# Decay steps on a ring of their own, with output, projections and taps placed among them

## Time and profile before

| | us |
|---|---|
| median of 3 runs | 1593.89 (1591.78 to 1598.0) |
| the profiled execution | 1599.31 |
| its span, first to last instruction | 1597.2 |
| TensorE busy | 1466.8 (92%) |
| VectorE busy | 1269.4 (79%) |
| ScalarE busy | 966.6 (61%) |
| GpSimd busy | 654.2 (41%) |

### The profile page before, as it was taken

How to read it: one execution, slowest core, us unless ns; L and a number is a source line. 1 busy time by engine, 2 the same in 40 slices (tenths; PEclk the granted TensorE clock), 3 DMA queues, 4 the chain that set the end, 5 groups by cost and what they waited for, 6 DMA issues and landing times.

```text
span 1597.2 us, 29712 instructions
## 1 busy us (share of the span) xinstructions
PE 1466.8 (92%) x9736; PEld 1143.2 (72%) x9736; DVE 1269.4 (79%) x2138; ACT 966.6 (61%) x1729; POOL 654.2 (41%) x554
## 2 busy tenths in 40 slices
PE   6799999799999789999879999877699999999979
PEld 5666666666766666666576676545598998998979
DVE  2788888698899788989779889943568988998954
ACT  3665666566566566656375656542267888887840
POOL 0134344133447524435814344834024544454530
PEclk7899999999999999999999999977769999999989
DMA  5376567466667755667847667713168989998858
GB/s 189 130 220 218 195 209 242 130 227 209 214 220 249 231 184 195 222 207 240 265 139 232 219 204 233 253 39 108 38 185 282 298 288 300 297 299 276 255 195 268
DMA packets 239686, 343.55 MB, mean 215 GB/s; under 512 B 20761, under 2 KB 191399, under 8 KB 238512
## 3 DMA queue, kind: packets, MB, share of 16 engines
q1 hardware_dynamic: 226096, 299.48, 59.4%
q0 software_dynamic: 13440, 42.19, 7.3%
HBM read 177.65 MB, written 172.30 MB: 219 GB/s over the span
## 4 chain that ended last, share of the span: by engine, by line
PE 64%; DVE 16%; issue 7%; ACT 5%; SPq 3%; DMA 2%; another core or an unknown queue 2%; POOL 1%; DVEq 0%; ACTq 0%; POOLq 0%
PE bank L451 12%; PE bank L618 11%; PE bank L453 10%; PE bank L452 10%; PE bank L629 6%; DVE e L1144 4%; PE bank L817 3%; PE bank L605 3%; DVE m L1185 2%; PE bank L793 2%; ACT e L880 2%; PE bank L763 2%; DVE e L1181 1%; DVE ew_lo L1077 1%
## 5 line engine op out<-in xcount | busy, mean ns | idle before, releaser
L1542 POOL TENSOR_TENSOR ssq<-ssq,ysq 128x512 f32<-128x512 f32 x128 | 167.8, 1311 | 428.7 <-ACT ysq L951 427.2
L1144 DVE SCALAR_TENSOR_TENSOR e<-bank,scal,e 128x511 f32<-128x511 f32 (+2 forms) x384 | 286.2, 745 | 35.2 <-ACT e L946 26.2
L1625 POOL DMA_INDIRECT outputs<-hsw,x_rows x160 | 181.6, 1135 | 238.0 <-DVE hsw L1488 185.7
L451 PE MATMUL bank<-h_hi,wi_hi 128*128 128x512 f32 x512 | 229.8, 449 | 33.2 <-issue 15.1
L618 PE MATMUL bank<-e,wn 128*128 128x512 f32 x512 | 247.6, 607 | 12.3 <-DVE e L1181 12.3
L1529 POOL TENSOR_TENSOR wi_lo<-wi,wi_hi 128x512 fp32r<-128x512 f32 x128 | 164.8, 1288 | 107.8 <-ACT wi_hi L828 107.8
L452 PE MATMUL bank<-h_lo,wi_hi 128*128 128x512 f32 x512 | 206.5, 403 | 0.0
L453 PE MATMUL bank<-h_hi,wi_lo 128*128 128x512 f32 x512 | 206.4, 403 | 0.0
L946 ACT ACTIVATE e<-bank,scal 128x512 f32<-128x512 f32 x128 | 99.4, 777 | 165.0 <-PE bank L453 163.4
L959 ACT ACTIVATE e<-e 128x512 f32<-128x512 f32 x128 | 80.7, 630 | 170.6 <-DVE e L1144 170.0
L1077 DVE TENSOR_TENSOR ew_lo<-ew,ew_hi 128x864 fp32r<-128x864 f32 x160 | 168.5, 1053 | 14.8 <-ACT ew_hi L828 8.1
(11 more groups left out here) (232 smaller groups left out, 3444.5 us busy)
## 6 DMA issues: line engine op xcount, KB each, us to landing
grouped<-zeros_out SPq DMA_DIRECT2D x256, 520.0 KB
ew<-expert_w SPq DMA_DIRECT2D x160, 432.0 KB
wi<-in_w SPq DMA_DIRECT2D x128, 256.0 KB
x_rows<-grouped SPq DMA_DIRECT2D x160, 130.0 KB
wo<-out_w SPq DMA_DIRECT2D x128, 128.0 KB
got<-outputs SPq DMA_DIRECT2D x16, 768.0 KB, 4.3
seg_wb<-seg_const POOLq DMA_DIRECT2D x4, 2048.0 KB, 8.3
seg_wa<-seg_const POOLq DMA_DIRECT2D x4, 2048.0 KB
```

Source lines behind the costliest of these rows:

```text
L451: mm(out, w_hi, x_hi, start=first, stop=False)
L1144: v.scalar_tensor_tensor(dst[:, d:], src[:, 0:SEQ - d], taps(TAPS - 1 - d), dst[:, d:], ALU.mult, ALU.add).then_inc(S[done], 1)
L1542: g_.tensor_tensor(ssq[:, :], ssq[:, :], ysq[:, :], ALU.add).then_inc(S["ssq_done"], 1)
L1625: g_.indirect_dma_start(outputs, bass.IndirectOffsetOnAxis(x_rows[:, i % XD, EMB:EMB + 1].bitcast(U32), 0), y_rows[:, i % YD, :], None, bo ...
```

## The change

- The decay steps get a ring of three: banks 6, 2 and 3, and for the exps the buffers `seg_e`, which are the two halves of `m` and `xt`. They no longer touch `ebuf`. Step 0 on ScalarE waits for the last head products of the batch before (`ssm`), steps 1 and 2 on TensorE for `xt_done` and `y_skip`.
- Slot 33 of a batch (last y: its square on ScalarE and the last output product on TensorE) moves into the next batch's steps, before step 3. Square sums stay before step 5, without the wait for VectorE's reading, which moves to before step 8. `gather_out` moves to before step 6.
- Pair 0's x projection runs before step 6 (TensorE), its first tap before step 8 (ScalarE), its three taps before step 10 (VectorE), its gate projection before step 10. In batches 1 to 3 the state products are before step 14 and the mask before step 18; in batch 0 both come after the steps.
- Pair 1 as well: cast of its weights before step 11, x projection before step 21, first tap before step 24, taps before step 27.
- The weights of the next batch's pairs 0 and 1 are loaded, and pair 0's cast and split, in the last slots of the batch before; in batch 0 pair 0's cast is before step 3.
- `seg_wb` is loaded in slot 31 and waits for three of the four send buffers.
- In batch 0 TensorE's steps wait for all six B/C taps.

The core of the diff:

```diff
-SEG_BANKS = (6, 0, 1, 2, 3, 7, 4, 5)
+SEG_RING, SEG_BANKS = 3, (6, 2, 3)
+SEG_OUT, SEG_SUMS, SEG_HID, SEG_GATHER, SEG_TAP0, SEG_SQUARE, SEG_TAPS, SEG_GATE = 3, 5, 6, 6, 8, 8, 10, 10
+SEG_NEXT_IN, SEG_G, SEG_MASK, SEG_NEXT_HID, SEG_NEXT_TAP0, SEG_NEXT_TAPS = 11, 14, 18, 21, 24, 27
-SEGMENTS_AT = 28
+SEGMENTS_AT, SECOND_SEGMENTS_AT = 28, 31
...
+            seg_e = (m[:, 0:2, :, :].rearrange("p t h l -> p (t h l)"), m[:, 2:4, :, :].rearrange("p t h l -> p (t h l)"),
+                     xt[:, :, :].rearrange("p t l -> p (t l)"))
...
             # SP
-                for par in range(2):
-                    load_in(b, par, par)
+                if b == 0:
+                    for par in range(2):
+                        load_in(b, par, par)
                 for j in range(PAIRS):
                     if j + 2 < PAIRS:
                         load_in(b, j + 2, j % 2)
+                    elif b + 1 < BATCH:
+                        load_in(b + 1, j + 2 - PAIRS, j % 2)
...
             # TensorE, segment
-                if u >= RING:
-                    pe.wait_ge(S["seg_exp"], n - RING + 1)
+                if u == 1:
+                    pe.wait_ge(S["xt_done"], START["xt_done"] + b * PAIRS)
+                if u == 2:
+                    pe.wait_ge(S["y_skip"], START["y_skip"] + b * PAIRS)
+                if u >= SEG_RING:
+                    pe.wait_ge(S["seg_exp"], n - SEG_RING + 1)
...
             # TensorE, a batch (hidden and gating are the two projections, cut out of slot)
+                pe.wait_ge(S["bc_taps"], 2 * (TAPS - 1) * (b + 1))
...
                 for u in range(CHUNK):
+                    if u == SEG_OUT and b:
+                        slot(b - 1, PAIRS + 1, 1, do_hid=False, do_in=False, do_mid=False, do_out="last")
+                        beside(b - 1, PAIRS + 1)
+                    if u == SEG_SUMS and b:
+                        pe.wait_ge(S["xhat"], (BATCH if b == 1 else BATCH + b - 1) * KE)
+                        square_sums(b - 1)
+                    if u == SEG_HID:
+                        hidden(b, 0, 0)
+                    if u == SEG_GATE:
+                        gating(b, 0, 0)
+                    if u == SEG_G and b:
+                        state_products(b)
+                    if u == SEG_NEXT_HID:
+                        hidden(b, 1, 1)
                     segment(b, u)
+                if b == 0:
+                    state_products(b)
                 beside(b, 0)
+                pe.wait_ge(S["seg_exp"], (b + 1) * CHUNK)
+                slot(b, 1, 1, do_hid=False, do_out="")
...
             # ScalarE
                 for u in range(CHUNK):
+                    if u == SEG_OUT:
+                        if b:
+                            slot(b - 1, PAIRS + 1, 1, do_tap=False, do_in=False, next_in=False, take_out=False)
+                            beside(b - 1, PAIRS + 1)
+                        else:
+                            take_in(b, 0, 0)
+                    if u == SEG_GATHER and b:
+                        gather_out(b - 1)
+                    if u == SEG_TAP0:
+                        first_tap(b, 0, 0)
+                    if u == SEG_NEXT_IN:
+                        take_in(b, 1, 1)
+                    if u == SEG_NEXT_TAP0:
+                        first_tap(b, 1, 1)
                     segment(b, u)
...
             # VectorE
+                    if u == SEG_SQUARE and b:
                         mean_square(b - 1)
+                    if u == SEG_TAPS:
+                        slot(b, 0, 0, do_mid=False, finish=False)
+                    if u == SEG_MASK and b:
+                        mask(b)
+                    if u == SEG_NEXT_TAPS:
+                        slot(b, 1, 1, do_mid=False, finish=False)
                     segment(b, u)
+                if b == 0:
+                    mask(b)
...
             # GpSimd
-                    for t in range(HD):
+                    for t in range(3):
                         pool.wait_ge(S[f"sent{t}"], 16 * TOP_K * max(0, b - 1))
...
-                    slot(b, j, j % 2, next_in=j < PAIRS - 1, finish=j > 1)
+                    slot(b, j, j % 2, next_in=j < PAIRS - 1 or j == PAIRS - 1 and b + 1 < BATCH, finish=j > 1)
```

More of the change, by code:

```diff
@@ L275, in seg_bank @@
         def seg_bank(u):
-            return bank[SEG_BANKS[u % RING]]
+            return bank[SEG_BANKS[u % SEG_RING]]
         def seg_step(b, u):
@@ L586, in beside, with hidden, gating, slot @@
                     i.then_inc(S["rank_mm"], 1)
-            def slot(b, j, par, do_in=True, do_mid=True, do_out="mid"):
+            def hidden(b, j, par):
                 g = b * PAIRS + j
                 x = tokens(b)
[L592 to L599, removed]
+                pe.wait_ge(S["wi_lo"], START["wi_lo"] + g + 1)
+                pe.wait_ge(S["taps"], START["taps"] + (TAPS - 1) * g)
+                for k in range(KE):
+                    w = slice((KE + k) * P, (KE + k + 1) * P)
+                    i = split_mm(p_hid[:, :], wi_hi[:, par, w], wi_lo[:, par, w], h_hi[:, k, x], h_lo[:, k, x],
+                                 k == 0, k == KE - 1)
+                i.then_inc(S["hid"], 1)
+            def gating(b, j, par):
+                g = b * PAIRS + j
+                x = tokens(b)
+                pe.wait_ge(S["silu_g"], START["silu_g"] + g)
+                for k in range(KE):
+                    w = slice(k * P, (k + 1) * P)
+                    i = split_mm(p_gate[:, :], wi_hi[:, par, w], wi_lo[:, par, w], h_hi[:, k, x], h_lo[:, k, x],
+                                 k == 0, k == KE - 1)
+                i.then_inc(S["gate"], 1)
+            def slot(b, j, par, do_hid=True, do_in=True, do_mid=True, do_out="mid"):
+                g = b * PAIRS + j
+                if do_hid:
+                    hidden(b, j, par)
                 if do_mid:
@@ L607, in slot @@
                 if do_in:
[L608 to L613, removed]
+                    gating(b, j, par)
                 if do_out:
@@ L654, in _, with state_products @@
             dt_turn(0)
[L655 to L679, removed]
+            def state_products(b):
+                pe.wait_ge(S["attn_scaled"], b * KE)
                 pe.wait_ge(S["bc_silu"], 2 * b + 2)
@@ L692, in _ @@
                     beside(b, j)
-                slot(b, PAIRS, 0, do_in=False)
+                slot(b, PAIRS, 0, do_hid=False, do_in=False)
                 beside(b, PAIRS)
-                slot(b, PAIRS + 1, 1, do_in=False, do_mid=False, do_out="last")
-                beside(b, PAIRS + 1)
+            slot(BATCH - 1, PAIRS + 1, 1, do_hid=False, do_in=False, do_mid=False, do_out="last")
+            beside(BATCH - 1, PAIRS + 1)
             def shared_rows(n):
@@ L1015, in _ @@
-                beside(b, PAIRS + 1)
+            slot(BATCH - 1, PAIRS + 1, 1, do_tap=False, do_in=False, next_in=False, take_out=False)
+            beside(BATCH - 1, PAIRS + 1)
             def shared_silu(u):
@@ L1387, in _ @@
                 for j in range(1, PAIRS):
-                    slot(b, j, j % 2, finish=j > 1)
+                    slot(b, j, j % 2, do_in=j > 1, finish=j > 1)
                     beside(b, j)
```

80 lines of the change are left out of this document (39 added, 41 removed).

## The result

The changed kernel takes 1602.68 us (median of 20 runs, 1598.29 to 1606.06), the kernel before 1593.76 (20 runs on the same chip). The ratio is 1.0047, with a 95% interval of 1.0033 to 1.0061, or +7.5 us (+5.3 to +9.7). A ratio with its interval need not be the quotient of the two medians (which lie 8.9 us apart here), and slow executions (8 of 35 of the kernel before and one with later square sums, both in the second group of experiments) are left out of the ratios but not of the medians. The change of 7.5 us is no change by the 0.5% bound and lies on the slow side of it. The profiled execution took 1598.6 us (span 1596.5, mean granted clock 0.955; before 0.949), less than all but one of the timed runs. So the two spans (1597.2 and 1596.5) hardly differ and can't show the timed difference. They do show where the time moved.

A forecast was written before the change was run, and what follows sets the result against it. The prediction took TensorE to bound the slots, leaving only batch 0's start and three boundaries to change. Batch 0 +7.0 and boundaries -4.1 give +2.9 us: 1602.2 for the profiled execution, 1597 for the median, range 1583 to 1609.

The forecast's parts named there:

- The forecast sum: Whole kernel: batch 0 +7.0 us and the three boundaries -4.1 us, together +2.9 us.
- three signs set for a wrong forecast: A boundary's last exp before A + 27 or after A + 33 (A: last head products' end); batch 0 losing under 4 us.
- The sign for TensorE's slow clock behind the square sums: Boundaries: TensorE's 2 us wait before square sums may drop its clock through projection and steps 6 to 8; +2.6 us counted.
- The 1 us left in the third for its drain: Boundary 3: 1 us kept in its 42.3 us forecast because its drain had run at the slow clock before.
- GpSimd's add: Boundaries, before the square sums: the last add of squares, slowed beside VectorE's steps, takes over 2 us, ending at 6.5.
- The 4.2 us that the prediction had set aside: Whole time lower by this if GpSimd isn't slowed beside VectorE: batch 0 1.5 less, each boundary 0.9 less.
- The wait of the first step: Batch 0: the first decay step waits for all six B/C taps, +3.2 us.
- the wait for the split before step 6: Batch 0: pair 0's projection waits for GpSimd's 2.76 us split; VectorE stands from 55.2 to 58.7.
- The second pair's part: Steps and tail: its taps add 2.3 us to VectorE's phase and take about as much from the tail; nothing by itself.
- The small rival: The second pair's part pays no gain in the tail: +2 us a place lost, 1605 us; chance 0.05.
- The short ring: Rival: three slots put TensorE's inserts in line among the steps, 2.5 us in each of four places, 1607 us; chance 0.25.
- The tails could have won: Rival: shorter boundary tails outweigh batch 0's loss, boundaries -13 and batch 0 +4 us, 1585 or 1581 us; chance 0.2.

The follow-up runs named there:

- second group of experiments: Kernel before (1588.67 us) and changed kernel (1593.42) timed again, beside the changed kernel with later square sums (1586.30) and a combined variant (1577.87), on one chip.
- the last group: Both kernels, unaltered, profiled twice more on one chip: 1560.40 and 1573.75 us before, 1567.30 and 1568.13 changed, one time each.
- The removal of everything: Changed kernel with all of batch 0 as before (no inserts among its steps, no B/C wait, ring of three kept): 1559.05 us, ratio 0.9976 to the kernel before.
- the last kernel: Changed kernel with batch 0 as before, pair 1 back in its slot and later square sums: 1577.87 us, ratio 0.9936 to the kernel before.
- the first comparison: The changed kernel against the kernel before, 20 runs each on the same chip: 1602.68 against 1593.76 us, ratio 1.0047.
- first and third group: First: changed kernel without B/C wait, batch 0 as before, pair 1 back, its taps late (1559.05 to 1571.20 us). Third: both kernels reprofiled (1560.40 to 1573.75).
- the kernel with late taps: Changed kernel with only VectorE's three taps of pair 1 moved behind m and xt of pair 0: 1571.20 us, ratio 1.0019 to the kernel before.

## Why the prediction was right, and where its steps were not

**The time.** 1597 was forecast and 1602.7 measured, inside the range, with no change by the 0.5% bound. The forecast sum of +2.9 us stands against +1.6 us to the mark in the profiled runs and +7.5 in the timed runs. The mechanism was right: batch 0 costs more than the boundaries give back. None of the three signs set for a wrong forecast came (last exps 30.7, 30.9 and 30.2 us behind the last head products, batch 0 8.1 longer). That the sum came so close is partly luck: over the four profiled runs each, batch 0 cost 2.6 more than forecast, the boundaries gave 2.5 more and the slots, set at nothing, 1.5.

**Boundaries.** Forecast 40.8, 41.3 and 42.3, measured 41.85, 41.5 and 40.5. VectorE's first step came at 2.65 (forecast 2.7). The last exps were through at 329.33, 30.7 us behind the mark (forecast 30.2), and the tail took 11.2 (forecast 10.6). The sign for TensorE's slow clock behind the square sums was right in two of three boundaries: 0.63 us rows in the first and second, where TensorE had stood 1.09 and 1.12 us, none in the third, where it had stood 1.98. So the length of this one wait doesn't tell whether the clock falls. The 1 us left in the third for its drain was not spent.

**GpSimd's add, a step that failed.** I had it over 2 us long and done at 6.5. It took 1.26 us and was done at 5.5 in the first boundary (6.4 in the third, where GpSimd came to it late from its stores). The square it waits for came on time, and VectorE's steps beside it became longer instead. GpSimd's rows of the changed kernel:
```profile
54.17 1.28 POOL L1571 TENSOR_TENSOR wi_lo<-wi,wi_hi 128x512 fp32r<-128x512 f32 x1 [8.62 <-ACT wi_hi L854]
...
302.89 1.26 POOL L1584 TENSOR_TENSOR ssq<-ssq,ysq 128x512 f32<-128x512 f32 x1 [5.04 <-ACT ysq L982]
```
Two steps take 1.19 us together and took 1.67 beside the add (303.42 above) and 1.81 beside the split (54.61). TensorE's wait for the square sums was 1.09, 1.12 and 1.98 us, where 2 was forecast. The same misjudged the split in batch 0 (2.76 forecast, 1.28 measured). The row of 2.76 us isn't one that repeats each time either. The same split amid the same steps of the kernel before took 2.72 and 2.73 us in two further profiled runs, but 1.27 in the first of the last group, and there VectorE's 32 steps took 17.24 us instead of 16.22:
```profile
62.89 1.27 POOL L1530 TENSOR_TENSOR wi_lo<-wi,wi_hi 128x512 fp32r<-128x512 f32 x1 [17.92 <-ACT wi_hi L829]
```
```profile
48.42 17.24 DVE L1158 SCALAR_TENSOR_TENSOR el<-e,consts 128x256 f32<-128x256 f32 x32
```
So one of the two engines pays, and the forecast had taken one case of two for the price. The 4.2 us that the prediction had set aside for an operation that isn't slowed were not gained as a whole, since VectorE lost part of what GpSimd kept. In that run TensorE stood 3.06 us before pair 0's projection instead of 4.54 and ran it at 0.39 us a matmul instead of 0.63, and batch 0 took 34.7 us instead of 37.7 to 38.9.

**Batch 0.** Forecast +7.0, measured +8.1. The wait of the first step was put at +3.2 and the first step came 3.6 later (52.63 against 48.16, less 0.85 of a later start). The removal of the wait gave 5.35, not 3.2, because with it goes the wait for the split before step 6 too (above). The forecast had priced that wait apart, at 3.5 us of standing; 2.4 were measured (0.30 and 1.44 of standing, 0.63 in longer steps). TensorE stands 6.94 us before its first step, and starts at 1.2 GHz, as forecast:
```profile
49.41 0.55 PE L530 MATMUL bank<-at_hi,seg_wb 128*128 128x256 f32 x1 [6.94 <-issue]
49.76 0.42 PE L531 MATMUL bank<-at_lo,seg_wb 128*128 128x256 f32 x1
```
Without the wait its matmuls also take 0.41 us from the seventh on, so its clock is not what the wait costs. The removal of everything gave 9.2. The last exp ended 33.5 us behind the start of the B/C taps (forecast 33.4), and the tail took 13.6 (forecast 12.6): the missing 1 us is there, where TensorE, after standing 5.37 us, took 4.8 us for the state products and the mean of batch 1 (forecast 3.4).

**The second pair's part.** It was priced at nothing, "its taps add 2.3 us to a phase that VectorE sets and take about as much from a tail", with a rival of +2 a place. The small rival, put at 0.05, was right. The two parts of the forecast, a phase of 30.2 us and a tail of 10.6, held all the same, since the taps were counted in the phase; wrong was what the tail would be without them. Taking it back gave 2.4, 3.7 and 1.4 in the boundaries and 2.3 in batch 0. Moving the taps alone gave 2.8, 1.6 and 1.2. From the last exp the tail took 10.4 to 11.2 us in the changed kernel and 10.4 to 11.3 with the taps back in it. So VectorE's 2.96 us of standing are what the taps leave behind, and in the tail they cost nothing. Had I written down VectorE's idle rows of my own forecast tail (7.4 to the head products, with `m` and `xt` as its only work, 1.9), it would have been visible.

**The two large rivals.** The short ring did not put the inserts in line: from step 9 on VectorE stood once in each boundary (0.41 to 0.43 us, before step 24), so TensorE's gate, state products and second projection were hidden as forecast; in batch 0, where mask and state products aren't among the steps, the second projection showed with 1.03 us. The tails could have won: the last kernel, with the same ring and pair 0 among the steps, is 0.64% faster than before.

**What stays open.** Of the timed +7.5 us, the profiled runs show +1.6 to the mark. A further +1.9 (means over four each, 45.7 against 43.8 for the start of the B/C taps) lies in the load of `consts` (means 7.6 against 5.7). It landed after 5.55 to 6.12 us in all four of the kernel before and after 6.12 to 10.70 in the ten of the changed kernel and its variants, four of them above 10.5, although its instruction is the same. Why isn't shown. The rest may lie behind the mark, whose length differs by 10 us between runs of one kernel; over four profiled runs each its mean is 1.0 us shorter for the changed kernel, so that it is longer there isn't shown. About 4 of the 7.5 us have no place.

## What to carry to other kernels

When work moves from a tail into a loop whose engines are all nearly full, ask for each piece on which engine the tail really waits: a piece taken from an engine that stands in the tail anyway gains little and is paid for in the loop. A consumer behind a chain of three engines (here square, add, sums) is to be placed several steps after its producer, since four steps later took 6.5 us out of three boundaries and cost two constants. Treat the first pass of a loop by itself: here all of the loss was in batch 0, where there was no drain to hide anything behind.

## What the runs showed of the hardware

**GpSimd beside VectorE: either of them can be the one that waits.** In the changed kernel, where VectorE had just been idle and GpSimd's operation started 0.4 to 0.5 us ahead of its step, GpSimd kept its 1.26 to 1.28 us and VectorE's next two steps took 0.5 to 0.6 us more. The same in the kernel without the B/C wait, where VectorE came straight from the last B/C tap:
```profile
49.17 1.27 POOL L1577 TENSOR_TENSOR wi_lo<-wi,wi_hi 128x512 fp32r<-128x512 f32 x1 [3.17 <-ACT wi_hi L861]
```
```profile
49.45 1.99 DVE L1199 SCALAR_TENSOR_TENSOR el<-m,consts 128x256 f32<-128x256 f32 x2
```
The Trainium skill (SBUF — State Buffer, section on SBUF's two separate sides) calls the shared pair of ports an exclusive lock that goes to whoever starts first, while the other fully blocks. Here that agrees: the two steps lost 0.80 us of the 0.99 that the split still ran. The other way round agrees too, in the tail of the changed kernel's boundary 1, where VectorE's product of two SBUF operands had started at 333.77, 0.09 us ahead of the split:
```profile
333.86 1.74 POOL L1571 TENSOR_TENSOR wi_lo<-wi,wi_hi 128x512 fp32r<-128x512 f32 x1 [18.74 <-ACT wi_hi L854]
```
But the order of starts doesn't settle every case. In boundary 3 VectorE's step started 0.34 us ahead of GpSimd's add, GpSimd kept its 1.28 us, and VectorE's two steps took 1.4 us more:
```profile
807.42 2.57 DVE L1192 SCALAR_TENSOR_TENSOR el<-m,consts 128x256 f32<-128x256 f32 x2 [0.38 <-ACT m L908]
```
```profile
807.76 1.28 POOL L1584 TENSOR_TENSOR ssq<-ssq,ysq 128x512 f32<-128x512 f32 x1
```
Nor amid a run of steps without gaps. In the kernel before, the split of batch 0 began 0.36 us into a step both times, and took 2.76 us in one profiled run, with three steps that began behind it at their usual 0.66 to 0.68 us, and 1.27 us in another, where the step behind it took 1.64. What decides in these cases isn't shown.

**A wait of 19 us in the untouched part, in some groups of runs.** In the first comparison and in the second group of experiments, ScalarE stood 19 to 20.5 us in the shared expert on something outside the profile's queues, in both kernels. In the first and third group it didn't. ScalarE in the changed kernel of the second group:
```profile
1098.49 0.60 ACT L1063 ACTIVATE hsw<-bank 128x512 f32<-128x512 f32 x1 [8.94 <-issue]
...
1119.60 0.59 ACT L1063 ACTIVATE hsw<-bank 96x512 f32<-96x512 f32 x1 [19.07 <-remote]
```
Where it is missing, ScalarE stands 2.1 to 2.2 us before the same instruction. This is most of the difference between 518 to 531 and 538 to 555 us behind the mark. What it is isn't shown.

**A stretch at 1.2 GHz that comes or stays away.** Windows of the start of the experts, of the changed kernel in the second group and of the kernel with later sums beside it:
```profile
1160.00:1190.00 30.00, 29.93 (x191) 28.80 (x191) 18.37 (x36) 16.79 (x35) 10.00 (x9) 0.62 0.63 186
```
```profile
1157.00:1187.00 30.00, 28.97 (x262) 26.34 (x262) 27.04 (x53) 24.56 (x52) 15.02 (x13) 1.00 0.91 288
```
TensorE is equally busy and does 191 against 262 matmuls. The profiled runs with such a stretch (before and changed in the first comparison, changed in the second group, and shorter ones in the kernel with late taps and in the second of before in the last group) are the ones that are long behind the mark in their group; that the stretch alone makes them long isn't shown. The kernel before, on one chip, came out at 1584 to 1589 us seven times and at 1595 to 1599 five times, so two single runs 10 us apart say nothing here.
